# Building dense edge matrices: next one-hots first, extra steps in twos, offsets loaded elsewhere

## The chip, the cores and the metric

The kernel runs on one core of a Trainium2 chip. The metric is the device time of one execution in microseconds (us); the figure for the kernel before is the median of three executions. The engines are named as in the profile: PE is TensorE (PEld its weight loads), DVE VectorE, ACT ScalarE, POOL GpSimd, SP the engine that issues the block transfers. A "q" behind a name (DVEq) is the engine's sequencer, which handles registers, branches and waits and hands work to the engine.

## What is computed

Four graph layers in a row on 6250 nodes with 64 features and 200000 edges that are sorted by destination. Each layer gathers neighbours and sums them per destination; between the layers stands a layer norm:

```python
x = _layernorm(x + L0(x, src, dst, W, b))          # Chebyshev, three propagations
x = _layernorm(x + L1(x, edge_index, edge_attr_64, ...))   # MLP on edges
x = _layernorm(x + L2(x, src, dst, edge_weight, gamma))    # two weighted sums, hyperbolic norm
x = _layernorm(x + L3(x, edge_index, ...))         # one propagation
# a propagation: segment_sum(x[src], dst); a weighted one: segment_sum(weight[:, None] * x[src], dst)
```

## The kernel before, in words

So that the propagations can be matrix products, the kernel first builds two dense matrices from the edge list: counts of edges (`dense_c`) and sums of edge weights (`dense_w`), both nodes by nodes. This stage, `build_dense`, is what the change touches. It runs on five engines at once.

**The tiling.** A source node is split into a high part (50 values) and a low part (125 values). Five destinations and the 50 high parts make the 250 keys of a group; there are 1250 groups. Two groups are a block (QUAD = 2), two blocks a unit (UNIT = 4): 313 units, the last with one block. Up to 256 edges of a group are read as two columns of 128 at most: the first 128 are prepared ahead in `firsts`, all others come in extra steps. As destinations with low numbers have far more edges than those with high ones, the first units have dozens of extra steps and the last 141 units have one in all.

**VectorE** (from line 925). `one_hots` (line 930) compares keys with a running number and writes the one-hot matrices of the keys and low parts; `products` (line 937) multiplies the low part's one-hot by the weight, which is split into three bf16 parts. `unit` (line 949) does this for the first columns of a unit: one `one_hots` for both blocks, two `products`. Then for each block `more` (line 941) runs once per extra step: `one_hots`, then `products`. Extra steps go in twos over two buffers, x = 2h and 2h + 1. The number of extra steps of a block is known only at run time: the offsets of the blocks lie in `offs_sb`, and `offs_of` (lines 399 and 392) loads five of them into registers once for every two units (line 966), ahead of both units.

```python
dve.wait_ge(first_used, u * pairs + pairs)      # line 951: TensorE is through with unit u - 2
...
dve.wait_ge(quad_taken, s + 2)                  # line 943: GpSimd has step s ready
dve.wait_ge(more_used, s + 1)                   # line 944: TensorE is through with step s - 2
```

**TensorE** (from line 1649). For the first columns of a unit it multiplies one-hots of low parts with one-hots of keys (`counts_of`, line 1653: 4 matmuls of 250 columns) as soon as the one-hots are there and ScalarE has emptied the bank, then key one-hots with the weighted low parts (`weights_of`, line 1661: 24 matmuls of 125 or 126 columns in two halves of 12, each behind one of the two `products`). An extra step is 2 and 12 of these, added to the same bank. It too loads five offsets ahead of each two units (line 1697). The counts one-hots of a unit's extra steps start only after its 24 products, as PE takes all this in program order.

**ScalarE** (from line 1412). Five blocks are a batch. For each batch it loads five offsets (line 1414), then for every block waits until TensorE is through with it and copies the bank out (lines 1424 and 1425). A ring of four blocks lies between TensorE and ScalarE. **SP** sends each finished batch to HBM (line 506). **GpSimd** (from line 641) picks the columns of each extra step into a ring of eight (line 655) and loads 16 offsets per batch.

Two sets of buffers matter: `first_planes` has two buffers (units u and u + 1), `more_planes` four (two for each block of a unit). `first_used` counts blocks, `more_used` counts steps, whatever the buffer.

Of the kernel before, what the change touches and what calls it, by code (L numbers as in the profile page):

```python
# [31 lines left out]
QUAD = 2  # L32
BLOCKS = GROUPS // QUAD
BATCH = 5
UNIT = 2 * QUAD
UNITS = -(-GROUPS // UNIT)
QRING = 8
# [77 lines left out]
def gnn_kernel(nc, xT, src, dst, weight, eaT, consts, counts, small, mats, wide, gamma_h, out):  # L115
# [9 lines left out]
    with ctx:  # L125
# [273 lines left out]
        def offs_of(eng, block, n):  # L399
            return loads(eng, offs_sb[0:1, ds(block, n)], 0, BLOCKS * COLS)  # L400
# [317 lines left out]
        def _(dve):  # L718
# [205 lines left out]
            def build_dense():  # L924
# [13 lines left out]
                                           low.unsqueeze(1).to_broadcast([P, 3, LO, QUAD]),  # L938
                                           weights.unsqueeze(2).to_broadcast([P, 3, LO, QUAD]), ALU.mult)

                def more(s, x):
                    quad = quads[:, ds(s & (QRING - 1), 1), :, :].rearrange("p s k t -> p (s k) t")
                    dve.wait_ge(quad_taken, s + 2)
                    dve.wait_ge(more_used, s + 1)
                    one_hots(more_planes[:, x, :], 1, quad[:, 0:3, :]).then_inc(more_hots, 1)
                    dve.wait_ge(more_hots, s + 1)
                    products(more_planes[:, x, :], 1, 0, quad[:, 3:6, :]).then_inc(more_products, 1)

                def unit(u, v, offs):
                    plane, pairs = first_planes[:, v, :], UNIT // QUAD  # L950
                    dve.wait_ge(first_used, u * pairs + pairs)
                    one_hots(plane, pairs, firsts[:, 0, ds(u * pairs, pairs), :, :].rearrange("p b k t -> p (b k) t")).then_inc(first_hots, 1)
                    dve.wait_ge(first_hots, u + 1)
                    for h in range(pairs):
                        products(plane, pairs, h, firsts[:, 1, ds(u * pairs + h, 1), :, :].rearrange("p b k t -> p (b k) t")).then_inc(first_products, 1)
                    dve.wait_ge(more_used, offs[0] + SLOTS)
                    dve.sem_inc(mores_begun, 1)
                    for h, (begin, past) in enumerate(zip(offs, offs[1:])):
                        with dve.If(past > begin):
                            with dve.Fori(begin, past, 2) as s:  # L960
                                more(s, 2 * h)
                                with dve.If(past > s + 1):
                                    more(s + 1, 2 * h + 1)

                with dve.Fori(0, UNITS // 2) as i:
                    offs = offs_of(dve, i * 4, 5)
                    for v in range(2):
                        unit(i * 2 + v, v, offs[2 * v:2 * v + 3])
                unit(UNITS - 1, 0, offs_of(dve, BLOCKS - 1, 2))
                end()  # L970

            def begin_rounds():
# [407 lines left out]
        def _(act):  # L1380
# [31 lines left out]
            def batch(n, j, turn):  # L1412
                nth, slot, b0 = j // BATCHES // 2, j // BATCHES % 2, j % 2
                past = offs_of(act, n * BATCH + 1, BATCH)
# [13 lines left out]
                C.activation(degp[0:LO, ds(n * SPAN, SPAN), :], dense_out[0:LO, b0, :, 0:2 * WCOLS:2 * WCOLS - 1], ACT.Copy).then_inc(degs_moved, 1)  # L1428

            with act.Fori(0, STREAMS // 4) as i:  # L1430
                for j in range(4 * BATCHES):
                    batch(i * (4 * BATCHES) + j, j, i)
            for j in range(BATCHES):
                batch((STREAMS - 1) * BATCHES + j, j, STREAMS // 4)
# [113 lines left out]
        def _(pe):  # L1548
# [102 lines left out]
            def build_dense():  # L1651
# [24 lines left out]
                def unit(u, v, offs):  # L1676
                    plane, blocks = first_planes[:, v, :], len(offs) - 1
# [10 lines left out]
                    with pe.If(offs[blocks] > offs[0]):  # L1688
# [11 lines left out]
                unit(UNITS - 1, 0, offs_of(pe, BLOCKS - 1, 2))  # L1700
                end()

            def dense_pass(l):
# [231 lines left out]
```

## Time and profile before

| | us |
|---|---|
| median of three executions | 6696.05 (6693.28 to 6703.47) |
| the profiled execution | 6737.52 |
| its span | 6735.8 |
| the build in it | 193 to 1992 |

The profile is of one execution. Its first part lists what each engine was busy with, the second the share of busy time in 40 slices, the fifth the costliest groups of instructions. A line in a view is that of the kernel's text. In the build, DVE works on lines 930 and 937, with the output tile T for the first columns and X for extra steps; PE works on lines 1653 and 1661 with the same tiles as inputs. A time line gives the start, the length, the engine and the line of instructions in order of time, with the idle time before one in brackets and what ended it.

### The profile page before, as it was taken

How to read it: one execution, taken by the hardware profiler on the slowest of the kernel's cores; microseconds unless marked ns; L12 is line 12 of the kernel's file. 1: busy time of each engine (PE TensorE's matmuls, PEld its weight loads, DVE VectorE, ACT ScalarE, POOL GpSimd, SP SyncE). 2: the span in 40 equal slices, each digit the busy share in tenths (PEclk: the TensorE clock that was granted, in tenths of full speed). 3: DMA queues.
4: the chain of work that ended last, by engine and by line, in shares of the span. 5: the costliest groups of instructions: out<-in, count | busy, mean ns of one | idle time of the engine just before them, and what ended most of it. 6: DMA issues, size and time to landing. Idle time of an engine off the chain costs nothing.

```text
span 6735.8 us, 125070 instructions
## 1 busy us (share of the span) xinstructions
PE 4407.9 (65%) x39288; PEld 3374.0 (50%) x39289; DVE 2743.6 (41%) x4741; ACT 1043.5 (15%) x2060; POOL 2010.8 (30%) x2919
## 2 busy tenths in 40 slices
PE   1788888777669999625555555555555567657475
PEld 0566666666559899523333333333333343323275
DVE  8877777665551111323333333333333320020323
ACT  1012223355550000100000000000000000000100
POOL 2433332211000000055656656565656510000000
PEclk6899999988888999755555555555555569989887
DMA  2012333456766898352222222222222259969575
GB/s 74 9 56 71 105 105 112 127 176 218 221 215 267 345 377 348 121 98 61 61 60 61 61 61 61 61 61 61 61 60 61 61 199 418 371 284 418 230 291 194
DMA packets 443170, 1061.56 MB, mean 158 GB/s; under 512 B 127013, under 2 KB 285543, under 8 KB 414216
## 3 DMA queue, kind: packets, MB, share of 16 engines
q1 hardware_dynamic: 390985, 1003.20, 41.7%
q0 software_dynamic: 52096, 57.38, 4.2%
q8 instruction: 30, 0.49, 0.0%
q14 instruction: 59, 0.48, 0.0%
HBM read 815.58 MB, written 244.81 MB: 157 GB/s over the span
## 4 chain that ended last, share of the span: by engine, by line
PE 23%; issue 19%; DVE 19%; another core or an unknown queue 16%; DMA 9%; DVEq 6%; ACT 4%; ACTq 2%; SPq 1%; POOLq 1%; POOL 0%
PE banks L1627 12%; DMA T<-dense_w 8%; DVE X L930 4%; PE banks L1661 3%; DVE T L930 3%; PE banks L1712 2%; DVEq L392 2%; DVE WORK L1048 1%; ACTq L392 1%; DVE WORK L1032 1%; DVE WORK L1046 1%; PE banks L1653 1%; DVEq L930 1%; PE banks L1599 1%
## 5 line engine op out<-in xcount | busy, mean ns | idle before, releaser
L695 POOL DMA_INDIRECT WORK<-table,idx x1568 | 1523.2, 971 | 1880.2 <-DVE idx L1054 875.5
L1627 PE MATMUL banks<-WORK,T 125*128 125x192 bf16 (+1 forms) x10000 | 834.4, 247 | 61.8 <-DVE WORK L1098 61.8
L1627 PEld LDWEIGHTS banks<-WORK,T 125*128 125x128 bf16 (+1 forms) x10000 | 832.0, 99 | 64.2 <-issue 47.5
L1588 PE MATMUL banks<-W1c,WORK 128*128 128x128 f32 x1568 | 474.3, 429 | 463.3 <-issue 461.8
L1712 PE MATMUL banks<-T,WORK 125*64 125x391 f32 (+1 forms) x3200 | 575.3, 500 | 228.1 <-DMA T<-dense_w 186.2
L1584 PE MATMUL banks<-T,WORK 128*128 x1568 | 275.5, 293 | 639.3 <-issue 319.8
L1588 PEld LDWEIGHTS banks<-W1c,WORK 128*128 128x128 f32 x1568 | 382.5, 320 | 504.0 <-issue 503.8
L655 POOL TENSOR_TENSOR T<-T 128x6 f32 x1182 | 365.3, 331 | 837.1 <-DVE X L937 694.3
L1661 PE MATMUL banks<-X 128*128 128x125 bf16 x7092 | 549.2, 226 | 62.9 <-DVE X L937 57.6
L1661 PE MATMUL banks<-T 128*128 128x125 bf16 (+1 forms) x7500 | 576.6, 239 | 0.2 <-DVE T L937 0.2
L1661 PEld LDWEIGHTS banks<-T 128*128 128x128 bf16 x7500 | 538.6, 120 | 51.1 <-DVE T L937 42.4
L1661 PEld LDWEIGHTS banks<-X 128*128 128x128 bf16 x7092 | 460.2, 116 | 201.8 <-DVE X L937 192.2
L1584 PEld LDWEIGHTS banks<-T,WORK 128*128 128x128 bf16 x1568 | 219.3, 140 | 669.9 <-issue 664.2
L1424 ACT ACTIVATE WORK<-banks 125x504 f32<-125x504 f32 x625 | 378.1, 605 | 1106.0 <-PE banks L1661 981.4
L1712 PEld LDWEIGHTS banks<-T,WORK 125*64 125x64 f32 x3200 | 253.0, 137 | 549.4 <-issue 432.2
L1597 PE MATMUL banks<-WORK 128*128 128x128 bf16 x1568 | 429.3, 274 | 118.3 <-DVE WORK L1048 113.2
L1482 ACT ACTIVATE WORK<-WORK 128x512 bf16<-128x512 f32 x196 | 123.5, 630 | 2386.2 <-issue 1301.2
L1599 PE MATMUL banks<-WORK 128*64 128x128 bf16 x1568 | 464.6, 296 | 5.3 <-issue 5.3
L1032 DVE TENSOR_TENSOR WORK<-banks,WORK 128x512 f32<-128x512 f32 x196 | 135.6, 692 | 745.8 <-remote 624.1
L930 DVE TENSOR_TENSOR T<-X,NORM 128x1500 bf16<-128x1500 bf16 x313 | 294.5, 941 | 331.6 <-issue 183.4
L1653 PE MATMUL banks<-T 128*128 128x250 bf16 x1250 | 221.5, 298 | 313.7 <-DVE T L930 193.6
L1017 DVE TENSOR_TENSOR ACC<-ACC,banks 128x128 f32 x196 | 55.9, 285 | 808.6 <-remote 776.4
(369 smaller groups left out, 4777.7 us busy)
## 6 DMA issues: line engine op xcount, KB each, us to landing
T<-dense_c SPq DMA_DIRECT2D x200, 1562.5 KB, 8.4
T<-dense_w SPq DMA_DIRECT2D x200, 782.0 KB, 10.3
T<-dense_w SPq DMA_DIRECT2D x200, 780.5 KB, 10.4
dense_w<-WORK SPq DMA_DIRECT2D x125, 1093.8 KB
WORK<-rel_rows SPq DMA_DIRECT2D x197, 256.0 KB
WORK<-in_eaT SPq DMA_DIRECT2D x392, 128.0 KB
dense_c<-T SPq DMA_DIRECT2D x13, 3125.0 KB, 14.8
dense_c<-ACC SPq DMA_DIRECT2D x12, 3125.0 KB, 15.1
```

Source lines behind the costliest of these rows:

```text
L655: last = nc.gpsimd.tensor_tensor(quads[:, ds(slot, 1), :, t].rearrange("p s k -> p (s k)"), lists[:, :, ds(at[t], 1)].rearrange("p k c -> ...
L695: nc.gpsimd.indirect_dma_start(out=g_sb[:, u, c * D:(c + 1) * D], out_offset=None, in_=table, in_offset=bass.IndirectOffsetOnAxis(ap=idx[: ...
L930: return V.tensor_tensor(plane[:, 0:pairs * HOTS].rearrange("p (k n t) -> p k n t", n=LO, t=QUAD), iota2[:, 0:LO, :].unsqueeze(1).to_broad ...
L1424: C.activation(dense_out[0:LO, b0, 2 * b:2 * b + 2, :], both[:, :, KEYS:KEYS + 2 * WCOLS], ACT.Copy)
L1584: T.matmul(z, lhsT, QW12[:, ds(at * 2, P)], start=c in (0, 2), stop=False, skip_group_check=True)
L1588: last = T.matmul(z_sums[:, v, 2 * c * P:2 * (c + 1) * P].rearrange("p (c h f) -> p h c f", c=2, f=D)[:, 0, :, :], ea_sb[:, v, c * P:(c + ...
L1597: T.matmul(banks[:, v, 0:P], parts[:, v, c, 0:2 * D], hots[:, v, c // 2, :, c % 2], start=c == 0, stop=False, skip_group_check=True)
L1599: last = T.matmul(banks[0:D, v, 0:P], parts[:, v, c, 2 * D:3 * D], hots[:, v, c // 2, :, c % 2], start=False, stop=c == CHUNKS - 1, skip_g ...
L1627: last = T.matmul(banks[0:cols, 2 * u + s, 0:3 * D], a_rows[:, u, h * WAYS + s * LO:h * WAYS + s * LO + cols], x123[:, h, :], start=h == 0 ...
L1653: T.matmul(banks[:, bank, 0:KEYS], lows_view(plane, h)[:, t, :], hots_view(plane, h)[:, t, :], start=begins, stop=False, skip_group_check= ...
L1661: last = T.matmul(banks[:, bank, to - low:to + LO + high], keys_view(plane, h)[:, t, j, :], plane[:, first - QUAD * low:past + QUAD * high ...
L1712: last = [T.matmul(banks[c * D:(c + 1) * D, 4 * h + j, 0:n], lt[:, y, :], aw_sb[0:LO, 4 * y + 2 * h + c, j * PIECE:j * PIECE + n], start=f ...
```

## The change

On VectorE the one-hots of unit u + 1 are issued ahead of the products of unit u, and the first unit's one-hots ahead of the loop. The load of the five offsets stands behind the products of the even unit, and the loop over two units thus begins with the next one-hots. Two extra steps are interleaved: both `one_hots`, then both `products`; a last odd step goes in an Else branch as before. On TensorE the offsets are loaded behind the even unit's matmuls of the first columns. On ScalarE one load brings the ten offsets of two batches in place of five for one.

```diff
-                def more(s, x):
-                    quad = quads[:, ds(s & (QRING - 1), 1), :, :].rearrange("p s k t -> p (s k) t")
+                def more_one_hots(s, x):
                     dve.wait_ge(quad_taken, s + 2)
                     dve.wait_ge(more_used, s + 1)
-                    one_hots(more_planes[:, x, :], 1, quad[:, 0:3, :]).then_inc(more_hots, 1)
+                    one_hots(more_planes[:, x, :], 1, quad_of(s)[:, 0:3, :]).then_inc(more_hots, 1)
+
+                def more_weights(s, x):
                     dve.wait_ge(more_hots, s + 1)
-                    products(more_planes[:, x, :], 1, 0, quad[:, 3:6, :]).then_inc(more_products, 1)
-                def unit(u, v, offs):
+                    products(more_planes[:, x, :], 1, 0, quad_of(s)[:, 3:6, :]).then_inc(more_products, 1)
...
+                def first_one_hots(u, v):
                     dve.wait_ge(first_used, u * pairs + pairs)
+                    one_hots(first_planes[:, v, :], pairs, ...).then_inc(first_hots, 1)
+                def first_weights(u, v):
                     dve.wait_ge(first_hots, u + 1)
                     for h in range(pairs):
+                        products(first_planes[:, v, :], pairs, h, ...).then_inc(first_products, 1)
+                def mores(offs):
                     dve.wait_ge(more_used, offs[0] + SLOTS)
                     dve.sem_inc(mores_begun, 1)
                     for h, (begin, past) in enumerate(zip(offs, offs[1:])):
                         with dve.If(past > begin):
                             with dve.Fori(begin, past, 2) as s:
-                                more(s, 2 * h)
                                 with dve.If(past > s + 1):
-                                    more(s + 1, 2 * h + 1)
+                                    for j in range(2):
+                                        more_one_hots(s + j, 2 * h + j)
+                                    for j in range(2):
+                                        more_weights(s + j, 2 * h + j)
+                                with dve.Else():
+                                    more_one_hots(s, 2 * h)
+                                    more_weights(s, 2 * h)
+                first_one_hots(dve.snap(0, min_val=0, max_val=0), 0)
                 with dve.Fori(0, UNITS // 2) as i:
-                    offs = offs_of(dve, i * 4, 5)
                     for v in range(2):
-                        unit(i * 2 + v, v, offs[2 * v:2 * v + 3])
+                        first_one_hots(i * 2 + (v + 1), 1 - v)
+                        first_weights(i * 2 + v, v)
+                        if v == 0:
+                            offs = offs_of(dve, i * 4, 5)
+                        mores(offs[2 * v:2 * v + 3])
...
             with act.Fori(0, STREAMS // 4) as i:
-                for j in range(4 * BATCHES):
-                    batch(i * (4 * BATCHES) + j, j, i)
+                for j in range(0, 4 * BATCHES, 2):
+                    past = offs_of(act, (i * (4 * BATCHES) + j) * BATCH + 1, 2 * BATCH)
+                    for k in range(2):
+                        batch(i * (4 * BATCHES) + (j + k), j + k, i, past[k * BATCH:])
...
                 with pe.Fori(0, UNITS // 2) as i:
-                    offs = offs_of(pe, i * 4, 5)
                     for v in range(2):
-                        unit(i * 2 + v, v, offs[2 * v:2 * v + 3])
+                        unit(i * 2 + v, v, 2)
+                        if v == 0:
+                            offs = offs_of(pe, i * 4, 5)
+                        mores(v, offs[2 * v:2 * v + 3])
```

## Rows read from the trace of the kernel before

**Rows 1.** The head of the page: the span.

```profile
span 6735.8 us, 125070 instructions
```

**Rows 2.** Busy time in three stretches: length, PE, PEld, DVE, ACT, POOL, PEclk, DMA share, GB/s.

```profile
193.00:603.00 410.00, 351.84 (x4256) 270.06 (x4256) 318.19 (x582) 58.28 (x114) 162.20 (x529) 0.98 0.14 41
603.00:1502.00 899.00, 738.48 (x8820) 600.00 (x8820) 646.06 (x1114) 320.12 (x641) 247.49 (x736) 0.94 0.39 122
1502.00:1992.00 490.00, 339.95 (x3943) 296.12 (x3943) 277.59 (x425) 294.25 (x620) 21.72 (x42) 0.89 0.69 215
```

**Rows 3.** The same stretches, line 930 (one-hots) alone, then line 937 (products).

```profile
193.00:603.00 410.00, 162.88 (x278) 0.98 0.14 41
603.00:1502.00 899.00, 323.59 (x484) 0.94 0.39 122
...
193.00:603.00 410.00, 165.12 (x304) 0.98 0.14 41
603.00:1502.00 899.00, 335.05 (x630) 0.94 0.39 122
```

**Rows 4.** Groups of DVE in the last stretch, 1502 to 1992: the first columns' one-hots.

```profile
L930 DVE TENSOR_TENSOR T<-X,NORM 128x1500 bf16<-128x1500 bf16 x141 | 132.8, 942 | 194.4 <-PE banks L1661 126.0 <-issue 68.0
```

**Rows 5.** Time line in the first unit, a long run of extra steps.

```profile
236.15 0.55 DVE L930 TENSOR_TENSOR X<-X,T 128x750 bf16<-128x750 bf16 x1
...
236.85 0.55 DVE L937 TENSOR_TENSOR X<-X,T 128x750 bf16<-128x750 bf16 x1
237.32 0.54 DVE L930 TENSOR_TENSOR X<-X,T 128x750 bf16<-128x750 bf16 x1
...
238.01 0.55 DVE L937 TENSOR_TENSOR X<-X,T 128x750 bf16<-128x750 bf16 x1
...
238.62 0.92 PE L1661 MATMUL banks<-X 128*128 128x125 bf16 x12
238.69 0.55 DVE L930 TENSOR_TENSOR X<-X,T 128x750 bf16<-128x750 bf16 x1
```

**Rows 6.** Time line at 626: two steps back to back on PE, and VectorE behind the first.

```profile
626.62 0.90 PE L1661 MATMUL banks<-X 128*128 128x125 bf16 x12
...
627.59 0.89 PE L1661 MATMUL banks<-X 128*128 128x125 bf16 x12
627.76 0.55 DVE L930 TENSOR_TENSOR X<-X,T 128x750 bf16<-128x750 bf16 x1 [1.35 <-PE banks L1661]
```

**Rows 7.** Time line of a unit with four extra steps, 630 to 638.

```profile
630.09 0.94 DVE L930 TENSOR_TENSOR T<-X,NORM 128x1500 bf16<-128x1500 bf16 x1
...
631.17 1.01 DVE L937 TENSOR_TENSOR T<-T,NORM 128x750 bf16<-128x750 bf16 x2
...
631.77 1.66 PE L1661 MATMUL banks<-T 128*128 128x125 bf16 x24
...
638.10 0.94 DVE L930 TENSOR_TENSOR T<-X,NORM 128x1500 bf16<-128x1500 bf16 x1 [0.87 <-issue]
```

**Rows 8.** Time line in the last stretch: units without extra steps.

```profile
1586.60 2.49 PE L1661 MATMUL banks<-T 128*128 128x125 bf16 x24
...
1593.03 0.94 DVE L930 TENSOR_TENSOR T<-X,NORM 128x1500 bf16<-128x1500 bf16 x1 [1.70 <-PE banks L1661]
...
1595.30 0.94 DVE L930 TENSOR_TENSOR T<-X,NORM 128x1500 bf16<-128x1500 bf16 x1
```

**Rows 9.** Loads of offsets (line 392), 1502 to 1992, then 193 to 603: min/median/max ns.

```profile
L392 DVEq TENSOR_LOAD <-X x70: 583/1974/3059, 1508.7 to 1988.5; - x70
L392 PEldq TENSOR_LOAD <-X x70: 579/1763/2896, 1509.2 to 1989.1; - x70
L392 ACTq TENSOR_LOAD <-X x56: 540/2264/5563, 1509.1 to 1984.9; - x56
...
L392 DVEq TENSOR_LOAD <-X x14: 583/596/2191, 192.1 to 601.0; - x14
L392 POOLq TENSOR_LOAD <-X x12: 1062/1068/3820, 192.0 to 601.4; - x12
```

More of the change, by code:

```diff
@@ L939, in products, with quad_of @@
                                            weights.unsqueeze(2).to_broadcast([P, 3, LO, QUAD]), ALU.mult)
-                def more(s, x):
-                    quad = quads[:, ds(s & (QRING - 1), 1), :, :].rearrange("p s k t -> p (s k) t")
+                def quad_of(s):
+                    return quads[:, ds(s & (QRING - 1), 1), :, :].rearrange("p s k t -> p (s k) t")
+                def more_one_hots(s, x):
                     dve.wait_ge(quad_taken, s + 2)
                     dve.wait_ge(more_used, s + 1)
-                    one_hots(more_planes[:, x, :], 1, quad[:, 0:3, :]).then_inc(more_hots, 1)
+                    one_hots(more_planes[:, x, :], 1, quad_of(s)[:, 0:3, :]).then_inc(more_hots, 1)
+                def more_weights(s, x):
                     dve.wait_ge(more_hots, s + 1)
-                    products(more_planes[:, x, :], 1, 0, quad[:, 3:6, :]).then_inc(more_products, 1)
-                def unit(u, v, offs):
-                    plane, pairs = first_planes[:, v, :], UNIT // QUAD
+                    products(more_planes[:, x, :], 1, 0, quad_of(s)[:, 3:6, :]).then_inc(more_products, 1)
+                pairs = UNIT // QUAD
+                def first_one_hots(u, v):
                     dve.wait_ge(first_used, u * pairs + pairs)
-                    one_hots(plane, pairs, firsts[:, 0, ds(u * pairs, pairs), :, :].rearrange("p b k t -> p (b k) t")).then_inc(first_hots, 1)
+                    one_hots(first_planes[:, v, :], pairs, firsts[:, 0, ds(u * pairs, pairs), :, :].rearrange("p b k t -> p (b k) t")).then_inc(first_hots, 1)
+                def first_weights(u, v):
                     dve.wait_ge(first_hots, u + 1)
                     for h in range(pairs):
-                        products(plane, pairs, h, firsts[:, 1, ds(u * pairs + h, 1), :, :].rearrange("p b k t -> p (b k) t")).then_inc(first_products, 1)
+                        products(first_planes[:, v, :], pairs, h, firsts[:, 1, ds(u * pairs + h, 1), :, :].rearrange("p b k t -> p (b k) t")).then_inc(first_products, 1)
+                def mores(offs):
                     dve.wait_ge(more_used, offs[0] + SLOTS)
@@ L1410, in _, with batch @@
             end()
-            def batch(n, j, turn):
+            def batch(n, j, turn, past):
                 nth, slot, b0 = j // BATCHES // 2, j // BATCHES % 2, j % 2
-                past = offs_of(act, n * BATCH + 1, BATCH)
                 for b in range(BATCH):
@@ L1430, in _ @@
             with act.Fori(0, STREAMS // 4) as i:
-                for j in range(4 * BATCHES):
-                    batch(i * (4 * BATCHES) + j, j, i)
+                for j in range(0, 4 * BATCHES, 2):
+                    past = offs_of(act, (i * (4 * BATCHES) + j) * BATCH + 1, 2 * BATCH)
+                    for k in range(2):
+                        batch(i * (4 * BATCHES) + (j + k), j + k, i, past[k * BATCH:])
             for j in range(BATCHES):
-                batch((STREAMS - 1) * BATCHES + j, j, STREAMS // 4)
+                batch((STREAMS - 1) * BATCHES + j, j, STREAMS // 4, offs_of(act, ((STREAMS - 1) * BATCHES + j) * BATCH + 1, BATCH))
             act.wait_ge(degs_moved, STREAMS * BATCHES)
@@ L1674, in more, with unit @@
                     last.then_inc(more_used, 1)
-                def unit(u, v, offs):
-                    plane, blocks = first_planes[:, v, :], len(offs) - 1
+                def unit(u, v, blocks):
+                    plane = first_planes[:, v, :]
                     pe.wait_ge(first_hots, u + 1)
@@ L1687, in unit, with mores @@
                         last.then_inc(first_used, 1)
-                    with pe.If(offs[blocks] > offs[0]):
+                def mores(v, offs):
+                    with pe.If(offs[-1] > offs[0]):
                         for h, (begin, past) in enumerate(zip(offs, offs[1:])):
@@ L1696, in build_dense @@
                 with pe.Fori(0, UNITS // 2) as i:
-                    offs = offs_of(pe, i * 4, 5)
                     for v in range(2):
-                        unit(i * 2 + v, v, offs[2 * v:2 * v + 3])
-                unit(UNITS - 1, 0, offs_of(pe, BLOCKS - 1, 2))
+                        unit(i * 2 + v, v, 2)
+                        if v == 0:
+                            offs = offs_of(pe, i * 4, 5)
+                        mores(v, offs[2 * v:2 * v + 3])
+                unit(UNITS - 1, 0, 1)
+                mores(0, offs_of(pe, BLOCKS - 1, 2))
                 end()
```

3 lines of the change are left out of this document (2 added, 1 removed).

## The prediction, made before the changed kernel ran

> **What bounds the kernel now.** The span is 6735.8 us [rows 1]; the profiled execution took 6737.52, 1.7 more than its span and 41 more than the median of 6696.05. I sum gains and losses in the profiled build and put the sum on the median. Only the build, from 193 to 1992, is touched. I read first where each engine is busy by stretch, then the time line inside a stretch, then the loads of offsets.
>
> The build has three kinds of stretch. A unit issues one `one_hots` and two `products`, an extra step one of each, so line 937's count less line 930's is the number of units: 304 - 278 = 26 units with 252 steps in the first 410 us, 630 - 484 = 146 units with 338 steps in the next 899 [rows 3], and 141 units with one step in the last 490 [rows 4]. In the first two stretches PE is busy 86% and 82%, DVE 78% and 72%, and ACT never over 36% [rows 2]. DVE's idle time is mostly its own sequencer: two steps take 2.54 us (236.15 to 238.69) for four instructions of 0.55, and PE begins 0.06 after each `products` ends (238.01 + 0.55 to 238.62) [rows 5]. A unit with four steps takes 8.01 us, of which 0.87 is the wait for the offsets [rows 7], so about 7.14 without. The bound there is VectorE's chain, with TensorE close behind it. In the last stretch nobody is full: PE 69%, DVE 57%, ACT 60%, at 3.48 us a unit (490 / 141). A unit on VectorE needs only 2.27 when nothing is in the way (1593.03 to 1595.30) [rows 8]; the rest goes to loads of offsets, median 1.97 on DVE and 2.26 on ACT [rows 9], and to waits for PE's products, 126 us of DVE's 194 idle [rows 4], which in turn wait for ScalarE's copies.
>
> **The order of VectorE's queue is the point.** Two waits change their place. `first_one_hots(u + 1)` waits until TensorE is through with unit u - 1, and now stands ahead of unit u's products. `more_one_hots(s + 1)` waits until TensorE is through with step s - 1, and now stands ahead of step s's products. Before, VectorE made the products while TensorE worked on the step before; now the products are queued behind the wait for it. The gain of interleaving is real only as long as TensorE is ahead.
>
> **Handoffs, from rows.** After TensorE's last matmul of a step VectorE starts 0.24 later (626.62 + 0.90 = 627.52 to 627.76); two steps of which both are ready follow on PE at 0.97 [rows 6]. Instructions of 0.55 on DVE can start 0.46 apart (two in 1.01 [rows 7]), an overlap of 0.09. A wait on its own result costs 0.14: one-hots of 0.94 to products takes 1.08 [rows 7].
>
> **Stretch one, 26 units.** In a run of steps the new cycle of a pair is: second one-hots 0.24 after PE, first products 0.46 later, 0.55 long, 0.06 to PE, 0.97 to the second step, 0.92 for that: 3.20 against 2.54 [rows 5, 6], +0.66. The first pair of a unit doesn't wait; it takes four starts at 0.46, about 1.9 against 2.33 (two steps at 0.70 + 0.47, 236.15 to 237.32 [rows 5]), -0.43. 252 steps are at most 126 pairs, less for odd blocks: I take 111, of which 26 are first. 85 x 0.66 = +56; 26 x 0.43 = -11. One-hots ahead of the other unit's products drop the self-wait and gain the overlap, 1.08 to 0.86: 26 x 0.22 = -6. The load on DVE is taken beside three instructions of 0.94, 0.55 and 0.55, if the sequencer runs ahead of the engine: 13 x 0.9 = -12. On PE the load now stands between the unit's 24 products and its extra steps, where before PE waited for one-hots anyway: 0.58 and about 0.19 to the next weight load, 13 x 0.77 = +10. Sum +37. Bounds: the wait hits no pair, -19; every pair, +65.
>
> **Stretch two, 146 units.** 39 have four steps, 32 three, 29 two, 23 one, 22 none, one has five (counted along its time line). Four steps (two and two): PE's 24 products and four steps of 0.97, its one wait for the second block's products, gives about 7.2, and 7.6 with half a PE load and its spacing; before, 7.14 and 8.01 in turns, mean 7.6. I take -0.2. With three steps or two, one pair or none stands in a block, so the new wait seldom bites: before 6.6 and 5.6, after 6.25 and 5.1 by the same terms. With one step 4.2 to 3.6. With none, 2.75 becomes 3.36, the cycle of the last stretch. 39 x -0.2, 32 x -0.35, 29 x -0.5, 23 x -0.6, 22 x +0.6 = -8 - 11 - 14 - 14 + 13 = -34. Bounds: -100, were TensorE's load covered as well and TensorE never waited (PE is busy 738 of 899 [rows 2]); +35, were VectorE's load not covered (73 x 0.95 given back).
>
> **Stretch three, 141 units.** Here the moved wait decides. From the last of a unit's 24 products: 0.24 to the one-hots, 0.86 to the products, 0.55, 0.06 to PE, 1.66 [rows 6 to 8]: 3.36 us a unit, and nothing in it can be prefetched. On every second unit PE's load comes in: issued 0.2 before the products end, median 1.76 [rows 9], 0.19 and 0.34 for the four count matmuls, it holds the products back until 2.1 after the last end, where they'd go at 1.71: +0.4 per two units. So 3.58, x 141 = 505 against 490: +15. ScalarE had two reasons to stall the others, five offsets at 2.26 for every batch and up to 5.56. Ten offsets in one load: POOL's 16 take 1.06 where five take 0.58 [rows 9], 0.044 each, so about 2.5 for ten; ScalarE needs 2.1 us a unit for copies and some 0.6 for the load, under 3.58, and only a load above some 3 us reaches PE. But VectorE can't catch up after a stall any more, having run units at 2.27 before. And the granted clock: some units' 24 products take 2.49 [rows 8] instead of 1.66 [rows 7], at 1.2 GHz instead of 2.4, in a stretch of clock 0.89 [rows 2]. Now PE pauses in every unit; if one unit in five is slow, 28 x 0.83 = +23. Together I put +25 for stalls and clock: +40 for the stretch. Bounds: -15 (loads short, clock as before) and +132 (every unit slow, 15 + 117).
>
> By the Trainium skill, "Runtime: NRT & Kernel Launch", section "Instruction fetch mechanics", a register load costs about 200 ns a register even in bulk. By it ScalarE's load of ten would take 1.0 more than one of five, not 0.2, and over 28 loads the sum could rise by up to 22 more. The row of 16 in 1.06 us speaks against it [rows 9].
>
> **The sum.** +37 - 34 + 40 = +43, on the median: 6739. The first one-hots ahead of the loop and the tail cost under 1 us. Transfers of the build fill 69% of the queues in the last stretch [rows 2], and nothing behind the build is changed.
>
> **Rivals.**
> 1. **Faster: TensorE's load is covered.** If TensorE's sequencer reaches the load while its matmuls still queue, the load costs nothing: -10 in stretch one, 73 x 0.8 = -58 in two, -15 in three, and with no more slow clock -25. 43 - 108 = -65: 6631. It decides if the load begins 0.6 us or more before the last weight load. For it: PE has a queue. Against: a matmul's weights are loaded at the pace of issue, and nothing in the chain of products runs ahead now. 0.17.
> 2. **Slower: VectorE's sequencer doesn't run ahead.** Then its load isn't hidden behind the one-hots and products, and the loop's return comes on top: some 0.9 per two units in stretches one and two: (13 + 73) x 0.9 = +77, less what PE's wait covers, +65 in all: 6804. Place: the first extra one-hots of an even unit. It decides if those start over 0.8 later than in an odd one. 0.17.
> 3. **Slower: the clock.** TensorE pauses 1.3 us in each unit of the last stretch and stays at 1.2 GHz for most: 141 x 0.83 = 117 in place of the 23 of my sum, 6833. For it: 2.49 us beside idle time already now. Against: pauses before slow units were often longer. 0.1.
> 4. **It evens out**, within 0.2% (13 us, about what a measurement of this kernel can tell): the middle gains 40 more. 0.11.
> 5. My sum: 0.45, its own range 6712 to 6785.
>
> Faster takes rival 1 and a little of 5: 0.19; same 0.11; slower 0.70. The range 6650 to 6835 leaves out most of rival 1 and the end of 3.
>
> **What would show it.** Right: in the first unit a pair of steps takes 3.2 us, and the first products of a pair start 0.46 after the second one-hots, which wait for PE; in the last stretch VectorE's one-hots wait for PE in every unit and follow at 3.4 to 3.7; the last stretch is 500 to 540 long, the first about 447, the second about 865. DVE's idle in front of one-hots is no more "issue". Wrong: a pair in a long run under 2.6, or units without steps under 3 us apart; then waits are not where I read them. A build under 1780 us makes the forecast wrong in sign.

## The result and the profile after

The changed kernel takes 6867.36 us (median of four executions; three lie between 6862.84 and 6868.69, the fourth was disturbed and is left out of the ratio) where the kernel before took 6696.72 in the same comparison: a ratio of 1.0251, 95% interval 1.0231 to 1.0271, 171 us slower (169 by the median of the three). The forecast was 6739 with a range up to 6835. The sign was right, the size was four times what I had worked out.

The build took 1799.4 us before and takes 1956.6 now, 157 more. The rest of the kernel is the same code and took 4742 us in the trace before and 4711 in this one: the execution profiled before lay 41 us above its median, so the two traces as a whole differ by 125 us only. The same three stretches of the build, first with all engines (columns as in [rows 2]), then DVE's groups and the loads of offsets:

```profile
span 6861.1 us, 125229 instructions
```

```profile
193.00:646.00 453.00, 340.27 (x4250) 279.20 (x4251) 303.32 (x584) 56.15 (x110) 143.30 (x529) 0.98 0.12 36
646.00:1547.00 901.00, 704.03 (x8830) 597.33 (x8827) 615.99 (x1115) 318.38 (x640) 258.44 (x742) 0.95 0.39 123
1547.00:2150.00 603.00, 377.04 (x3948) 312.99 (x3948) 263.66 (x424) 304.57 (x626) 15.97 (x37) 0.79 0.56 175
```

```profile
L930 DVE TENSOR_TENSOR T<-X,NORM 128x1500 bf16<-128x1500 bf16 x140 | 131.9, 942 | 338.8 <-PE banks L1681 330.5 <-issue 8.1
```

```profile
L392 ACTq TENSOR_LOAD <-X x65: 549/5371/10292, 192.3 to 2142.6; - x65
```

The first stretch is 43 us longer, the middle one 3, the last one 112 (from the first products of unit 0, 26 and 172; the windows are cut at whole microseconds). In the last stretch VectorE's idle time ahead of its one-hots went from 194 us, of which 126 waited for PE [rows 4], to 339, of which 331 do. ScalarE has half as many loads, but each takes 5.37 us at the median, where one of five offsets took 2.26 [rows 9]. The granted clock fell from 0.89 to 0.79.

The time line of the last stretch shows the cycle that the moved wait makes, without any stall in it:

```profile
1905.71 1.65 PE L1681 MATMUL banks<-T 128*128 128x125 bf16 x24 [0.78 <-DVE T L937]
...
1907.51 0.94 DVE L930 TENSOR_TENSOR T<-X,NORM 128x1500 bf16<-128x1500 bf16 x1 [1.40 <-PE banks L1681]
...
1908.37 1.00 DVE L937 TENSOR_TENSOR T<-T,NORM 128x750 bf16<-128x750 bf16 x2
...
1908.97 1.64 PE L1681 MATMUL banks<-T 128*128 128x125 bf16 x24 [1.13 <-DVE T L937]
...
1910.76 0.94 DVE L930 TENSOR_TENSOR T<-X,NORM 128x1500 bf16<-128x1500 bf16 x1 [1.40 <-PE banks L1681]
```

PE ends unit u - 1 at 1907.36, the one-hots of u + 1 follow at 1907.51, only then the products of u at 1908.37, PE takes them at 1908.97, and the next one-hots wait for its end: 3.25 us. Of the last stretch's one-hots none follow those before in under 3 us now; before, 66 of 140 did. And this is a stall behind a load of ScalarE's that takes 9.8 us, from 1888.67 to 1898.47; the row of the load stands first, then the time line behind it:

```profile
L392 ACTq TENSOR_LOAD <-X x1: 9807/9807/9807, 1888.7 to 1888.7; - x1
```

```profile
1899.84 0.60 ACT L1442 ACTIVATE WORK<-banks 125x504 f32<-125x504 f32 x1
1900.01 0.13 PEld L1673 LDWEIGHTS banks<-T 128*128 128x128 bf16 x2 [8.96 <-ACT T L1443]
...
1901.38 2.72 PE L1681 MATMUL banks<-T 128*128 128x125 bf16 x24
...
1904.25 0.94 DVE L930 TENSOR_TENSOR T<-X,NORM 128x1500 bf16<-128x1500 bf16 x1 [11.03 <-PE banks L1681]
```

PE waited 9 us for a bank and then ran its 24 products at 1.2 GHz, 2.72 us instead of 1.65; VectorE stood still for 11. Of the 140 units with 24 products 48 took over 2.2 us for them, 31 before; all 140 together took 283 us, 262 before.

In the first stretch a pair of extra steps takes 3.27 us (237.17 to 240.44) where it took 2.54 [rows 5]. The second one-hots (238.13) follow the end of PE's second step of the pair before (236.93 + 0.90 = 237.83):

```profile
236.93 0.90 PE L1681 MATMUL banks<-X 128*128 128x125 bf16 x12
237.17 0.55 DVE L930 TENSOR_TENSOR X<-X,T 128x750 bf16<-128x750 bf16 x1 [0.82 <-PE banks L1681]
...
238.13 0.55 DVE L930 TENSOR_TENSOR X<-X,T 128x750 bf16<-128x750 bf16 x1 [0.41 <-POOL T L655]
238.60 1.00 DVE L937 TENSOR_TENSOR X<-X,T 128x750 bf16<-128x750 bf16 x2
...
240.44 0.55 DVE L930 TENSOR_TENSOR X<-X,T 128x750 bf16<-128x750 bf16 x1 [0.84 <-PE banks L1681]
```

The bracket at 238.13 names GpSimd, but the wait was for PE. These are the one-hots of step 21 (counted from 0): GpSimd had 28 steps ready by then, while PE had finished exactly the 20 that they need, the last at 237.83. VectorE's sequencer passes its wait for PE (line 946) at 237.87 and the one for GpSimd 0.07 later.

### The profile page after: what moved, and what is told of

The parts are those of the page before. It is cut to its first block, busy times and chain, and to the rows that moved or that the text cites. A ratio compares the mean times of both kernels' runs of the same rounds, so it can differ in the third digit from the quotient of the medians.

```text
span 6861.1 us, 125229 instructions
## 1 busy us (share of the span) xinstructions
PE 4366.1 (64%) x39288; PEld 3383.2 (49%) x39289; DVE 2680.9 (39%) x4741; ACT 1048.7 (15%) x2060; POOL 2004.1 (29%) x2919
## 4 chain that ended last, share of the span: by engine, by line
PE 26%; another core or an unknown queue 18%; DVE 17%; issue 14%; DMA 9%; DVEq 5%; ACTq 4%; POOLq 3%; ACT 2%; SPq 1%; POOL 1%
PE banks L1647 12%; DMA T<-dense_w 8%; PE banks L1681 5%; ACTq L392 3%; PE banks L1737 2%; DVEq L392 2%; DVE WORK L1067 2%; DVE X L937 2%; DVE WORK L1051 1%; DVE X L930 1%; PE banks L1619 1%; DVE WORK L1054 1%; PE banks L1617 1%; DVE WORK L1065 1%
## 5 line engine op out<-in xcount | busy, mean ns | idle before, releaser
L1681 PEld LDWEIGHTS banks<-X 128*128 128x128 bf16 x7092 | 483.2, 116 | 270.8 <-DVE X L937 262.4
L1617 PEld LDWEIGHTS banks<-WORK 128*128 128x128 bf16 x1568 | 163.7, 104 | 854.4 <-issue 709.9
L1608 PE MATMUL banks<-W1c,WORK 128*128 128x128 f32 x1568 | 440.6, 431 | 197.8 <-issue 197.0
L930 DVE TENSOR_TENSOR X<-X,T 128x750 bf16<-128x750 bf16 x591 | 318.9, 551 | 336.3 <-PE banks L1681 147.1
## 6 DMA issues: line engine op xcount, KB each, us to landing
T<-dense_w SPq DMA_DIRECT2D x200, 782.0 KB, 10.3
```

Of the source, the lines that this page charges most:

```text
L930: return V.tensor_tensor(plane[:, 0:pairs * HOTS].rearrange("p (k n t) -> p k n t", n=LO, t=QUAD), iota2[:, 0:LO, :].unsqueeze(1).to_broad ...
L1608: last = T.matmul(z_sums[:, v, 2 * c * P:2 * (c + 1) * P].rearrange("p (c h f) -> p h c f", c=2, f=D)[:, 0, :, :], ea_sb[:, v, c * P:(c + ...
L1617: T.matmul(banks[:, v, 0:P], parts[:, v, c, 0:2 * D], hots[:, v, c // 2, :, c % 2], start=c == 0, stop=False, skip_group_check=True)
L1681: last = T.matmul(banks[:, bank, to - low:to + LO + high], keys_view(plane, h)[:, t, j, :], plane[:, first - QUAD * low:past + QUAD * high ...
```

## The experiments

The runs were made on other chips than the first, on which the kernel before takes between 6160 and 6167 us, or 6735 beside e13. So each time is given as a difference to the kernel before of the same comparison, and the stretches are read from the traces: from the first products of unit 0, 26 and 172 to the next mark, the last one to ScalarE's last copy of the build. The kernel before was traced on the first chip alone. That its stretches hold for the others rests on two things: the first stretch takes 409 in it, 411 in e2 and 410 in e7, which leave VectorE and TensorE as they were; and for each run the difference in time and that of the build agree within some 10 us, but for the change itself (171 and 157). All in us; the interval of a ratio is in the text.

| kernel | time | first | middle | last | build |
|---|---|---|---|---|---|
| before | | 409 | 899 | 491 | 1799 |
| the change | +171 | 452 | 902 | 603 | 1957 |
| e1 the change, ScalarE's old loads | +63 | 451 | 883 | 534 | 1868 |
| e2 ScalarE's ten offsets alone | +70 | 411 | 909 | 552 | 1872 |
| e3 next one-hots ahead alone | +37 | 402 | 871 | 562 | 1835 |
| e4 twos alone | +85 | 468 | 922 | 496 | 1886 |
| e5 loads of DVE and PE moved alone | -14 | 405 | 891 | 489 | 1784 |
| e6 one-hots behind the products, loads moved | -88 | 392 | 828 | 483 | 1703 |
| e7 ScalarE's load begins at a multiple of four | -19 | 410 | 893 | 473 | 1775 |
| e8 ScalarE's load earlier | -19 | 413 | 892 | 474 | 1778 |
| e9 e6 with eight values in fours | -126 | 392 | 822 | 456 | 1670 |
| e10 e3 with the one-hots behind the products | -51 | 399 | 850 | 489 | 1738 |
| e11 the change, ten offsets in fours | +67 | 453 | 892 | 528 | 1872 |
| e12 e9, PE's load not moved | -107 | 397 | 841 | 463 | 1701 |
| e13 e4's branches without its order | +99 | 448 | 946 | 495 | 1889 |
| e14 e9 with twos, odd step apart | +29 | 454 | 893 | 486 | 1834 |
| e15 e9, odd step apart, old order | -11 | 403 | 901 | 489 | 1794 |

**One part at a time.** e1 takes ScalarE's change back, e2 has it alone:

```diff
-                for j in range(0, 4 * BATCHES, 2):
-                    past = offs_of(act, (i * (4 * BATCHES) + j) * BATCH + 1, 2 * BATCH)
-                    for k in range(2):
-                        batch(..., past[k * BATCH:])
+                for j in range(4 * BATCHES):
+                    batch(i * (4 * BATCHES) + j, j, i)        # loads five itself
```

> The changed kernel with ScalarE's loads as before (five offsets for each batch). In the changed kernel the load of ten takes 5.36 us at the median against 2.26 for five, and a unit of the last stretch takes 4.27 us on average but 3.72 at the median. Theory 1 (ScalarE's long load stalls TensorE every fifth unit): the mean falls to the median, 141 x 0.55 = 78 us less, so about 6790. Rival (the waits moved on VectorE make up the whole loss): under 15 us less, 6852 or more.

> The kernel before with only ScalarE's change (ten offsets for two batches). Theory 1: each load takes 5.4 us or more, so a pair of batches costs ScalarE about 0.8 us more than before, and in one piece, which the ring of four blocks covers less: 15 to 60 us slower, 6712 to 6757. Rival (VectorE and TensorE catch up after each stall, as they run units at 2.27 us): within 10 us of before.

e1: ratio 1.0111 (1.0094 to 1.0128). The build falls by 88 us (the time by 108), 69 of it in the last stretch, where a unit goes from 4.27 to 3.78 us on average. e2: 1.0116 (1.0099 to 1.0133), build +73, more than expected. So ScalarE's ten offsets cost 70 us alone and 88 to 108 on top of the other parts, over half of the loss. Alone, the twos below cost more (85).

e3 is the kernel before with this alone (its `unit` split into the functions of the change, and the first unit's one-hots ahead of the loop):

```diff
                 with dve.Fori(0, UNITS // 2) as i:
                     offs = offs_of(dve, i * 4, 5)
                     for v in range(2):
-                        first_one_hots(i * 2 + v, v)
+                        first_one_hots(i * 2 + (v + 1), 1 - v)
                         first_weights(i * 2 + v, v)
                         mores(offs[2 * v:2 * v + 3])
```

> The kernel before with only the next unit's one-hots issued ahead of a unit's products; loads and extra steps as before. Theory 2 (the products are queued behind the wait for unit u - 1): in the last stretch units follow at 3.4 us or more, never at 2.27; with VectorE's load still on its path every second unit, the stretch takes 510 to 560 us instead of 490, the two stretches before it gain up to 0.22 us a unit: 6700 to 6740. Rival (the one-hots ahead are free and the loss lies in the loads): 5 to 40 us faster than before.

1.0055 (1.0039 to 1.0072). The last stretch is 562 us, at the edge of what I gave, the two before it are 36 shorter. e10 moves the one line behind `first_weights`:

> The kernel with the next one-hots alone (the third run, 37 us slower, last stretch 562 us), with one line moved: the next unit's one-hots behind this unit's products instead of ahead. Theory 2 (products queued behind a wait): the 37 us turn into a gain, last stretch at or under 491 us, the middle one 20 to 60 us under 899; 30 to 70 us faster than before. Rival (issuing a unit early is what costs): still slower than before.

0.9907 (0.9882 to 0.9932): 37 us slower has become 51 faster, and all parts of the expectation hold (last stretch 489, middle one 49 less). VectorE's groups of the last stretch, e3 first, then e10:

```profile
L930 DVE TENSOR_TENSOR T<-X,NORM 128x1500 bf16<-128x1500 bf16 x140 | 131.7, 941 | 296.5 <-PE banks L1676 282.8 <-issue 13.6
```

```profile
L937 DVE TENSOR_TENSOR T<-T,NORM 128x750 bf16<-128x750 bf16 x282 | 143.4, 551 | 155.7 <-issue 142.7 <-DVE T L930 5.9
L930 DVE TENSOR_TENSOR T<-X,NORM 128x1500 bf16<-128x1500 bf16 x140 | 131.6, 940 | 62.7 <-PE banks L1676 62.2
```

The wait for PE ahead of the one-hots falls from 283 us to 62. In e10 64 of 140 one-hots again follow in under 3 us; in e3, e1, e11 and the changed kernel none does. The order of two lines, with all the work the same, is worth 88 us (97 in the build).

e5 moves the loads alone, e6 moves them and puts the one-hots behind the products:

> The kernel before with only VectorE's and TensorE's loads of offsets moved behind the even unit's first columns. The changed kernel with ScalarE's old loads lost 69 us in its build, the next one-hots alone 35 and the twos alone 87, so if parts add up, this part gains 53: 6115 to 6140 on the chip whose kernel before took 6167 (ratio 0.991 to 0.996). Rival (TensorE's load now stands between a unit's products and its extra steps, as in my forecast): within 10 us of before.

> The loads moved as in the change, extra steps and ScalarE as before, and the next unit's one-hots issued behind the unit's own products instead of ahead of them. Theory 2 (the loss of the last stretch comes from products queued behind a wait): without that order the last stretch follows the old pace, units at 2.3 to 3.4 us, under 491 us; the stretches before gain 0.2 us a unit beside the moved loads: 30 to 90 us faster than before. Rival (one-hots a unit early cost by themselves, in buffers or clock): slower than before, as the next one-hots alone were.

e5: 0.9974 (0.9963 to 0.9985), 14 us faster, a miss for both readings: the parts don't add up. Beside the order ahead the moved loads seem to be worth more. In e1, which has both, the first extra one-hots come 0.4 us later behind a unit's products where VectorE's load stands between (even units) than where it doesn't (0.91 and 0.49 on average); in e5 they come 1.4 us later (1.41 and 0.02). So the load is better covered in e1. That this makes up all of the missing 38 us isn't shown. e6: 0.9857 (0.9841 to 0.9874), 88 faster, at the upper end. e12 puts TensorE's load back ahead of the unit in e9:

> The kernel of run e9 with TensorE's load left ahead of the unit, as before the change, VectorE's still moved. My forecast charged TensorE's moved load 0.8 us for every two units between the products and the extra steps. If so, this one is faster by 10 to 60 us. If TensorE waits for VectorE there anyway, or its load ahead of the count matmuls costs as much: within 10 us of e9.

0.9814 against e9's 0.9784: 20 us slower, 31 in the build, outside both readings and against my charge for it. In this kernel TensorE's load ahead of the unit is the worse place; with the one-hots ahead it wasn't tried by itself.

**What makes a load long.** In e7 the load begins at a number divisible by four, in e8 it stands ahead of the batch's last block:

```diff
-                past = offs_of(act, n * BATCH + 1, BATCH)
+                lead = (j * BATCH + 1) % 4
+                past = offs_of(act, n * BATCH + 1 - lead, BATCH + lead)[lead:]
```

> The kernel before with ScalarE's load for a batch beginning at an offset whose number is divisible by four, so five to eight values in place of five. In the trace before every fourth load takes 0.55 us (it begins at such a number), the three others 2.26. If the first number decides: all loads take 0.55 to 0.8 us, the sum of the 125 falls from 296 to about 90, the last stretch gains 20 to 60 us: 0.990 to 0.997 of before. If what decides is the batch's store that begins 0.7 us after the load does, or the count of values: loads of seven or eight take 3 us or more, and the time is the same or up to 20 us longer.

> The kernel before with ScalarE's load of the next batch's five offsets placed ahead of the waits for the batch's last block, so that it no longer begins with the store of a finished batch. If the store makes loads long: most take 0.6 to 1 us, and what is left hides in the wait for TensorE; the last stretch gains 20 to 60 us, 0.990 to 0.997 of before. If the first number decides alone: median 2.2 us as before, but hidden in part, 0 to 20 us gained.

e7: 0.9974 (0.9964 to 0.9983), e8: 0.9965 (0.9953 to 0.9978), 19 us each, no difference between them; the last stretch gains 18 and 17, just under what I gave. In e7 the sum of the loads is 161 us where it was 296, short of the 90 I gave; most loads of five and of eight values take 0.56, of six 0.76, of seven 1.6.

Both causes are real, and e8 separates them, since its load is away from the batch's store:

```profile
L392 ACTq TENSOR_LOAD <-X x125: 541/1134/5553, 194.0 to 1964.5; - x125
```

Of its 94 loads of five that begin elsewhere than at a multiple of four, 49 take 1.11 to 1.14 us, where in the kernel before such loads take 2.3 at the median: that is 0.22 a value. So four neighbours come at once if the load begins at a multiple of four, and what is left comes singly at about 0.2 each (six values 0.76 against 0.55 for five). The rest is the store: in the kernel before, its first packets stand 0.71 us behind the load's start, and a load that is still under way then becomes long (five values 2.3 instead of 1.12, seven 1.6). e9 and e11 test that: e9 reads eight values for each batch, e11 is the changed kernel with 12 or 16 values for its two batches.

```diff
+                lead = (j * BATCH + 1) % 4
+                past = offs_of(act, n * BATCH + 1 - lead, 8)[lead:]                                    # e9
+                    past = offs_of(act, ... * BATCH + 1 - lead, 12 if lead < 3 else 16)[lead:]         # e11
```

> The fastest kernel so far (next one-hots behind the products, loads moved, 88 us faster than before) with ScalarE's load for each batch beginning at a number divisible by four and always eight values. In the run with five to eight values, loads of five and of eight took 0.56, six 0.76, seven 1.6 us. If values come in fours and what is left one by one: the median is 0.56 us, the last stretch 10 to 30 us shorter than 483: 100 to 120 us faster than before. Rival (VectorE and TensorE set the pace there now): within 5 us of the kernel without it, 88 faster.

> The changed kernel with only ScalarE's load altered: it still serves two batches, but begins at a number divisible by four and brings 12 or 16 values. If the ten values were slow because they came one by one past the start of the store (5.36 us): the loads take 0.8 to 1.1 us, as GpSimd's 16 do alone, and the kernel stands at or under the changed kernel with the old loads, 50 to 65 us slower than before. Rival (ten values in one load are long in themselves, more values more so): 6 us or more a load and 160 or more slower.

ScalarE's loads in the changed kernel stand above; here e7, e11 and e9:

```profile
L392 ACTq TENSOR_LOAD <-X x125: 543/762/4628, 191.5 to 1960.5; - x125
```

```profile
L392 ACTq TENSOR_LOAD <-X x65: 560/1574/5461, 191.5 to 2057.2; - x65
```

```profile
L392 ACTq TENSOR_LOAD <-X x125: 541/553/3181, 191.2 to 1856.1; - x125
```

e11 brings more values than the change and takes 1.57 us where that takes 5.37 (I had said 0.8 to 1.1); with 1.0093 (1.0068 to 1.0117) its build stands 4 us from that of e1, which has the old loads. The length of the change's load comes from where it begins, and from the store that it thus meets. Whole fours don't guard a load that begins amid other packets: in e9 29 of the 125 still take 1.1 to 3.2 us, and VectorE's loads of five, which all begin at a multiple of four, take 1.97 at the median in the last stretch [rows 9]. e9: 0.9784 (0.9761 to 0.9807), 126 us faster than before (130 in the build) and so faster than both kernels; its last stretch is 27 us shorter than e6's. It is the fastest kernel of the study, though e6's 88 and e9's 126 come from different comparisons: in the builds the fours are worth 33 us.

**The twos.** e4 is the kernel before with the If, the Else and the interleaving:

> The kernel before with only the extra steps interleaved in twos. Theory 3 (the second one-hots of a pair wait for TensorE with the first products behind them): the first unit's pairs take 3.2 to 3.6 us instead of 2.54, the first stretch (to unit 26) takes about 45 us more, the middle stretch changes by less than 20, the last not at all: 6720 to 6760. Rival (interleaving gains the self-waits and costs nothing): 590 steps at up to 0.2 us less, 30 to 100 us faster.

1.0142 (1.0125 to 1.0159), 85 us, more than expected, and 23 of it in the middle stretch where I had seen little. e13 keeps the branches and gives the old order back:

```diff
                                     for j in range(2):
                                         more_one_hots(s + j, 2 * h + j)
-                                    for j in range(2):
                                         more_weights(s + j, 2 * h + j)
```

> The kernel with the twos alone (fourth run, 85 us slower), with its new branches (both steps inside the If, a single one in the Else) but each step's products right behind its own one-hots, as before. Theory 3 (the products are queued behind the second one-hots' wait for TensorE): the first unit takes 83 to 86 us instead of 105, the first stretch at most 415 instead of 468; what is left of the 85 us is the branches, up to 25 us. Rival (the added branches cost VectorE's sequencer 0.1 to 0.25 us a block and make up the loss): 50 us or more slower than before.

1.0151 (1.0133 to 1.0169): the rival held, and my theory alone can't explain e4. The branches by themselves cost 90 us of build:

```profile
237.24 0.55 DVE L930 TENSOR_TENSOR X<-X,T 128x750 bf16<-128x750 bf16 x1 [0.44 <-POOL T L655]
237.94 0.55 DVE L937 TENSOR_TENSOR X<-X,T 128x750 bf16<-128x750 bf16 x1
...
240.09 0.55 DVE L930 TENSOR_TENSOR X<-X,T 128x750 bf16<-128x750 bf16 x1 [0.44 <-POOL T L655]
```

A pair takes 2.85 us here (237.24 to 240.09), 2.54 before [rows 5], 3.27 in the change. By the rows of VectorE's sequencer the 0.31 is spent between the second products and the next one-hots, with the engine idle: some 0.19 for the jump past the Else, 0.06 for the If, which now stands there and not under a running instruction, and 0.07 for one more instruction for the waits. Units with one step in each block, where nothing is interleaved, take 6.2 us in e4 and 6.1 in e13, 5.85 before. The order (e4 against e13, which ran on different chips) costs 20 us in the first stretch and gives 24 back in the middle. e14 and e15 start from e9 and take the branch out of the loop:

```diff
+                        with dve.If(past > begin + 1):
+                            with dve.Fori(begin, past - 1, 2) as s:      # full pairs
+                                ...
+                        with dve.If((past - begin) & 1 > 0):             # one odd step
```

> On the kernel of run e9 (build 1670 us, 126 us faster than before): extra steps interleaved in twos as in the change, but the loop runs over full pairs without an If inside, and an odd last step stands behind it under an If of its own. The last run showed that the branch inside the loop costs 0.31 us a pair and all of the twos' 87 us, while the order by itself lost 20 us in the first stretch and won 24 in the middle. If the order is what it looks: the first unit takes 95 to 105 us, the first stretch 5 to 25 us more than 392, the middle stretch 0 to 40 less than 822. Rival (branches of a tail cost as much as the Else): 40 us or more slower than e9.

> The same loop over full pairs with the odd step apart, each step's products behind its own one-hots. If a branch inside the loop is what costs: the first unit takes 79 to 85 us (pairs at 2.3 to 2.55), the first stretch stays at or under 392, the middle one within 20 of e9's 822. Rival (the tail's test costs every block 0.2 us): the middle stretch is 40 us or more longer.

e14: 1.0043 (1.0026 to 1.006), e15: 0.998 (0.997 to 0.9989), both far behind e9. VectorE's rows of a pair, e14 first, then e15:

```profile
236.92 0.55 DVE L930 TENSOR_TENSOR X<-X,T 128x750 bf16<-128x750 bf16 x1 [0.77 <-PE banks L1681]
237.95 0.55 DVE L930 TENSOR_TENSOR X<-X,T 128x750 bf16<-128x750 bf16 x1 [0.48 <-POOL T L655]
238.41 1.00 DVE L937 TENSOR_TENSOR X<-X,T 128x750 bf16<-128x750 bf16 x2
240.18 0.55 DVE L930 TENSOR_TENSOR X<-X,T 128x750 bf16<-128x750 bf16 x1 [0.76 <-PE banks L1681]
```

```profile
236.11 0.55 DVE L930 TENSOR_TENSOR X<-X,T 128x750 bf16<-128x750 bf16 x1
...
238.66 0.55 DVE L930 TENSOR_TENSOR X<-X,T 128x750 bf16<-128x750 bf16 x1
```

e15's pairs are back at 2.55 in the long run, but every block pays for one more test, those without steps too: its middle stretch is 79 us longer than e9's, its last 34. For e15 the rival held. Between e15 and e14 stands only the order: +51 in the first stretch, -8 in the middle; I had given e14's first stretch 5 to 25 more than e9's, it is 62. Its pair takes 3.26 without any branch inside the loop, and e4's and the change's take 3.25 at the median with one. So in a long run the order by itself makes the whole of the change's pair, and the branch hides in the wait for PE; without the order the branch shows, at 2.85. Each is enough to make the first stretch longer (39 us for the branches in e13, 51 for the order in e14 against e15), and together they cost 59 (e4), not the sum. In the middle the branches cost 47 (e13). The gain of the order there that e4 and e13 showed (24) is small once the branch is gone. Interleaving with more buffers, so that the second one-hots need not wait, wasn't tried.

## Why the prediction was wrong

**Right.** The mechanism of the last stretch: none of its one-hots follow in under 3 us, the cycle is 3.25 us where I had 3.36, and e10 shows that the order of the queue makes it. The pair in a long run: 3.27 against 3.20, and e14 shows that the moved wait alone gives it; the first stretch was 43 us longer for 37 forecast. Rival 2 is out: by its own sign the first extra one-hots of an even unit would start over 0.8 us later than in an odd one, and they start 0.33 later (0.89 and 0.56 behind the products).

**Wrong, first: ScalarE's load of ten.** The step was "0.044 each, so about 2.5 for ten", by which only a load above some 3 us reaches PE; of the +25 for stalls and clock together 23 were clock, so 2 were left for the stalls. The 0.044 came from GpSimd's 16 values, which begin at a multiple of 16; the ten begin at 1, 11, 21 and so on. They take 5.37. The cost by e1 is 88 us of the build (69 in the last stretch, 19 in the middle, where I had charged none). With ScalarE's old loads the last stretch is 43 us longer than before, for 40 forecast, so this step makes 69 of the stretch's miss of 72. The Trainium skill's figure in "Runtime: NRT & Kernel Launch", section "Instruction fetch mechanics", of some 200 ns a register, which I weighed and set aside by that row, is given there for registers loaded from HBM; it is what single values cost here (five in 1.12 in e8). It does not hold for fours, where 16 took 1.06. The row and the page were both right, for different addresses. What I did not see in the trace before is that ScalarE's loads of five were already of two kinds, 0.55 and 2.26, one in four and three in four.

**Wrong, second: the middle stretch.** I summed -34, it was +3. Two parts were missing. The branches: e4 lost 23 us there (e13, with the branches and the old order, 47). And ScalarE's load: 10 us alone (e2), 19 on top of the rest (e1). What I had priced came out in sum: the next one-hots gave 28 (e3) and the moved loads 8 (e5), 36 for my 34. The single terms did not. By kind of unit, means in us (the one unit with five steps is left out):

| steps | units | before, as I had it | before | after | change forecast | change measured |
|---|---|---|---|---|---|---|
| 4 | 39 | 7.6 | 7.85 | 7.96 | -0.2 | +0.11 |
| 3 | 32 | 6.6 | 7.13 | 6.72 | -0.35 | -0.41 |
| 2 | 29 | 5.6 | 5.81 | 5.70 | -0.5 | -0.11 |
| 1 | 23 | 4.2 | 4.63 | 5.17 | -0.6 | +0.54 |
| 0 | 22 | 2.75 | 3.58 | 3.76 | +0.6 | +0.18 |

The largest miss is the term 23 x -0.6; with ScalarE's old loads (e1) such a unit takes 4.71. And my times before, worked out from single rows, were short for every kind. "With three steps or two, one pair or none stands in a block, so the new wait seldom bites" may hold of the wait, but the diff showed the If moved to the front and the Else; I costed them at nothing and named no cover. There was none: I had written myself that VectorE's idle time is mostly its sequencer. TensorE's moved load, charged in all three stretches, was a gain of 20 us where it was tried by itself (e12 against e9), which is nearer to rival 1 than to my sum.

**Right in size, wrong in its place: the clock.** I put +23 for one unit in five at the low clock. Of 140 units 48 took over 2.2 us for their products, but 31 did before; the sum grew from 262 to 283 us, 21. With ScalarE's old loads (e1) it is 260 with 28 such units, so in the whole change these 21 us go with the long loads and are part of the 69. e3 has the old loads and 49 such units, 283 us in all, so long loads aren't the only way to it; what decides stays open. Rival 3, with most units slow, did not come. Without clock and stalls my sum for the last stretch was +15 (by its own terms 3.36 + 0.2 = 3.56 a unit, +12), and e1 still has +43 there with none of it in the clock. So that e1 meets my +40 is in part luck; what makes up the other 28 isn't shown.

The parts don't add: the four alone come to +178 us by time (70 + 37 + 85 - 14), the whole to 171. This nearness is chance: by the builds they come to 180, the whole to 157, and e5, e14 and e15 show how far parts hide in each other.

## What to carry to other kernels

When instructions are moved up in an in-order queue, their waits move with them, and all that stands behind now waits too: put the work of the next unit behind that of this one, not ahead of it. Read every row of a load with its address and its number of values before it serves as a price for another. And where the sequencer is the bound, the time of a branch counts in full: an If and Else in VectorE's loop cost 0.31 us a turn here, over half of a 0.55 us instruction, and one more test for every block, with the loop rearranged, 112 us in the two later stretches (e15 against e9).

## What the runs showed of the hardware

A register load of offsets reads four neighbours at once if it begins at a number divisible by four (5 or 8 values 0.56 us, 16 in 1.06), single values at about 0.2 us (five that begin elsewhere 1.12, in e8). It is far longer when it is under way while the same program's store starts (five values 2.26, ten 5.37, up to 10.3). VectorE's taken jump past an Else took 0.19 us to the sequencer's next instruction, and the If and Else cost 0.31 a turn. And the chips differ outside the build: between its end and the kernel's, the traces show 4742 and 4711 us on the first chip, 4749 in e13, and 4161 to 4179 in all others, which ran on four more chips; the first stretch of the build, where its code is the same, takes 409, 411 and 410 on three of them. The stage that differs is the gathers of the second layer, which the kernel before starts at 2894 and ends at 5421 on the first chip, e5 at 2886 and 4847 on the other.
